# Transposing every second pair of attention rows in the scores' 64-row tiling, and scaling both layer-1 maxima with one product behind the reciprocal

## The reference

```python
sim = einsum('bihd,bjhd->bhij', q, k) * SCALE     # 112 x 375 per head
attn = softmax(sim, axis=-1)
out = einsum('bhij,bjhd->bihd', attn, v)
```

## Time and profile before

| | |
|---|---|
| median of 3 runs | 2443.48 us (2443.19 to 2444.84) |
| profiled execution | 2448.87 us, span 2447.0 us |
| busy share of the span | PE 97%, PEld 72%, DVE 68%, ACT 65%, POOL 67% |
| mean granted TensorE clock | 0.985 |
| attention pairs in all | 512 |

### The profile page before, as it was taken

The page is one execution under the profiler, slowest core; times in us unless marked ns, Lnnn a source line. Parts: engine busy times, 40 slices in busy tenths (PEclk is TensorE's granted clock), DMA queues, the critical chain, the costliest instruction groups (busy, mean ns, idle before and its releaser), DMA issues.

```text
span 2447.0 us, 58983 instructions
## 1 busy us (share of the span) xinstructions
PE 2369.9 (97%) x18734; PEld 1767.7 (72%) x18734; DVE 1658.4 (68%) x4412; ACT 1580.5 (65%) x4305; POOL 1648.5 (67%) x1894
## 2 busy tenths in 40 slices
PE   6999999999999999999999999999999999999578
PEld 5777777777777777777777777777777777777336
DVE  6666666776666667666666766666677666667775
ACT  4666666766666676666666766666676666666346
POOL 2666776666677766666776666677666666876507
PEclk9999999999999999999999999999999999999689
DMA  4100000000000000000000000000000000000202
GB/s 151 35 11 10 10 8 10 2 10 10 10 10 8 10 2 10 10 10 10 10 8 4 8 10 10 10 10 8 10 2 10 10 10 10 8 4 1 54 10 61
DMA packets 31196, 37.02 MB, mean 15 GB/s; under 512 B 3284, under 2 KB 29636, under 8 KB 31172
## 3 DMA queue, kind: packets, MB, share of 16 engines
q1 hardware_dynamic: 31172, 36.71, 5.1%
HBM read 29.36 MB, written 7.34 MB: 15 GB/s over the span
## 4 chain that ended last, share of the span: by engine, by line
PE 86%; ACT 5%; DVE 4%; issue 3%; POOL 1%; DMA 0%; ACTq 0%; POOLq 0%; DVEq 0%; SPq 0%
PE ps L334 24%; PE ps L395 15%; PE pt L405 14%; PE pa L417 5%; PE ps L378 5%; PE pa L452 5%; PE pa L432 4%; ACT prob L765 3%; PE pt L334 2%; PE pa L334 2%; PE pa L586 1%; PE pa L544 1%; DVE nmx L995 1%; PE pt L569 1%; PE ps L445 1%
## 5 line engine op out<-in xcount | busy, mean ns | idle before, releaser
L995 DVE TENSOR_REDUCE nmx<-ps 112x2 f32<-112x750 f32 x512 | 476.6, 936 | 204.1 <-PE ps L395 204.1
L1432 POOL TENSOR_TENSOR prob<-prob,rinv 112x375 f32<-112x375 f32 x512 | 404.2, 811 | 273.9 <-DVE rinv L1011 267.7
L1432 POOL TENSOR_TENSOR f1w_room<-f1w_room,rinv 112x375 f32<-112x375 f32 x512 | 404.8, 814 | 30.4 <-DVE rinv L1011 24.0
L727 ACT ACTIVATE room<-ps 128x375 f32<-128x375 f32 (+2 forms) x480 | 228.3, 489 | 272.2 <-PE ps L334 272.2
L986 DVE COPY probT<-pt 125x336 f32<-125x336 f32 x512 | 253.5, 495 | 100.0 <-PE pt L405 99.7
L727 ACT ACTIVATE probT<-pt 125x336 f32<-125x336 f32 x512 | 234.0, 457 | 109.0 <-PE pt L405 106.3
L405 PEld LDWEIGHTS pt<-ident,prob 112*125 112x125 f32 x1536 | 192.0, 189 | 130.3 <-issue 92.8
L405 PEld LDWEIGHTS pt<-ident,f1w_room 112*125 112x125 f32 x1536 | 197.9, 188 | 115.7 <-POOL f1w_room L1432 53.2
L1457 POOL TENSOR_TENSOR krs<-krs,nhalf 125x48 f32<-125x48 f32 x32 | 257.0, 8031 | 0.0
L405 PE MATMUL pt<-ident,prob 112*125 112x112 f32 x1536 | 239.6, 291 | 0.0
L405 PE MATMUL pt<-ident,f1w_room 112*125 112x112 f32 x1536 | 235.7, 287 | 1.6 <-DVE probT L986 0.9
(11 more groups left out here) (260 smaller groups left out, 5128.6 us busy)
## 6 DMA issues: line engine op xcount, KB each, us to landing
craw<-in_ctx SPq DMA_DIRECT2D x32, 375.0 KB, 3.1
xin<-in_x SPq DMA_DIRECT2D x32, 112.0 KB, 2.0
x_rows<-x SPq DMA_DIRECT2D x32, 112.0 KB, 1.9
out<-probT SPq DMA_DIRECT2D x16, 224.0 KB, 2.3
room<-x_rows SPq DMA_DIRECT2D x1, 2576.0 KB, 13.4
stage<-in_f1w SPq DMA_DIRECT2D x2, 1024.0 KB, 5.1
stage<-in_wk SPq DMA_DIRECT2D x1, 1024.0 KB, 7.8
stage<-in_wv SPq DMA_DIRECT2D x1, 1024.0 KB, 10.3
```

The source lines that it names most:

```text
L727: return act.activation(dst, src, ACT.Copy)
L995: top = dve.tensor_reduce(nmx[:, g:g + 2], ps[0:T, 2 * (i % 2):2 * (i % 2) + 2, 0:S], AX_X, ALU.max, negate=True)
L1432: pool.tensor_tensor(prob(i, n), prob(i, n), rinv[:, g:g + 1].to_broadcast([T, S]), ALU.mult).then_inc(s["normed"], 1)
```

## The change

Pairs with odd i and i+3 below the count (pairs 1, 3, 5, 7, 9, 11 of MIDDLE; 1 and 3 of OPENING and of CLOSING) are transposed by rows: each 112x125 piece becomes a transpose of its rows 0 to 63 into bank 0 and one of its rows 64 to 111 into bank 1, twelve transposes in place of six, behind a small bf16 product of one column. All waits stand ahead of that product: both copies of the pair before, and both heads' `normed`. ACT and DVE copy out one bank each as before, ACT 2x3x64 columns and DVE 2x3x48, both once all twelve are done. The other pairs stay as they are.

In layer 1 the two scalings become one 112x2 product (`max_scale`), which stands behind the reciprocal of the pair before in DVE's order and counts `maxed`; the maximum itself counts a new semaphore `top1`.

```diff
+        ROWS = ((0, 64), (64, T))
+        def by_rows(i, part):
+            return i % 2 == 1 and i + 1 + AHEAD < (G if part == MIDDLE else PAIRS)
...
             def turn(i, part, b):
+                if by_rows(i, part):
+                    pe.wait_ge(s["pT_even"], at(i, part, b))
+                    pe.wait_ge(s["pT_odd"], at(i, part, b))
+                    pe.wait_ge(s["normed"], 2 * at(i, part, b) + 2)
+                    pe.matmul(pt[:, 0, 511:512], identb[0:64, :], identb[0:64, 0:1], start=True, stop=True)
+                    for n in range(2):
+                        for t in range(KT):
+                            for bank, (r, e) in enumerate(ROWS):
+                                col = (n * KT + t) * (e - r)
+                                last = pe.transpose(pt[0:SK, bank, col:col + e - r],
+                                                    prob(i, n)[r:e, t * SK:(t + 1) * SK], ident[r:e, r:e])
+                                if n == 1 and t == KT - 1:
+                                    last.then_inc(s["pT"], 1)
+                    return
...
             def turned(i, part, b):
+                if by_rows(i, part):
+                    act.wait_ge(s["pT"], 2 * at(i, part, b) + 2)
+                    copy(probT[:, 2 * (i % 4):2 * (i % 4) + 2, :, 0:64],
+                         pt[0:SK, 0, 0:2 * KT * 64].rearrange("p (n k t) -> p n k t", n=2, k=KT))\
+                        .then_inc(s["pT_even"], 1)
...
-                if layer == 1:
-                    link(top)
-                    if p % 2 == 0:
-                        dve.wait_ge(s["q1_rstd"], b * 4 + (p // 2 + 1))
-                    for n in range(2):
-                        h = HEADS1[2 * p + n]
-                        top = dve.tensor_scalar(nmx[:, g + n:g + n + 1], nmx[:, g + n:g + n + 1], qrs[:, 2, h:h + 1],
-                                                None, ALU.mult)
-                top.then_inc(s["maxed"], 1)
+                top.then_inc(s["top1" if layer else "maxed"], 1)
+
+            def max_scale(i, part, b):
+                layer, p = pair_of(i, part)
+                if layer == 1:
+                    g, h = H + 2 * p, HEADS1[2 * p]
+                    assert HEADS1[2 * p + 1] == h + 4
+                    dve.wait_ge(s["top1"], b * PAIRS + (p + 1))
+                    if p % 2 == 0:
+                        dve.wait_ge(s["q1_rstd"], b * 4 + (p // 2 + 1))
+                    dve.tensor_tensor(nmx[:, g:g + 2], nmx[:, g:g + 2], qrs[:, 2, h:h + 5:4], ALU.mult)\
+                        .then_inc(s["maxed"], 1)
...
                     if i + 1 < count:
                         row_sum(i + 1, part, b)
+                    if i + AHEAD < count:
+                        max_scale(i + AHEAD, part, b)
```

More of the change, by code:

```diff
@@ L22 @@
 U8_EPS = 1e-8
-DVE_STEPS = 29
+DVE_STEPS = 21
 POOL_STEPS = 7
@@ L212, in xattn_ffn_kernel @@
             "x_in ctx_in cT_hi cT_lo k0_ready k0_sb v0_ready v0_sb var0 rstd0 xn0_ready xT0_ready xT0_sb "
-            "q0_ready q0_sb xbo_ready scores maxed exped recip normed pT pT_even pT_odd pv o_sb wo_ready x1_ready "
+            "q0_ready q0_sb xbo_ready scores top1 maxed exped recip normed pT pT_even pT_odd pv o_sb wo_ready x1_ready "
             "var1 rstd1 xq_ready diag_ready xqT_ready rb_ready xqT_sb rb_sb kv1_ready kv1_sb h_ready h_sb conv0 "
@@ L748, in turned @@
             def turned(i, part, b):
-                act.wait_ge(s["pT"], 2 * at(i, part, b) + 1)
-                copy(probT[:, 2 * (i % 4), :, :], pt[0:SK, 0, 0:KT * T].rearrange("p (k t) -> p k t", k=KT))\
-                    .then_inc(s["pT_even"], 1)
+                if by_rows(i, part):
[3 more added lines that the diff above has]
+                        .then_inc(s["pT_even"], 1)
+                else:
+                    act.wait_ge(s["pT"], 2 * at(i, part, b) + 1)
+                    copy(probT[:, 2 * (i % 4), :, :], pt[0:SK, 0, 0:KT * T].rearrange("p (k t) -> p k t", k=KT))\
+                        .then_inc(s["pT_even"], 1)
             def exps(i, part, b):
@@ L985, in turned @@
                 dve.wait_ge(s["pT"], 2 * at(i, part, b) + 2)
-                dve.tensor_copy(probT[:, 2 * (i % 4) + 1, :, :],
-                                pt[0:SK, 1, 0:KT * T].rearrange("p (k t) -> p k t", k=KT))\
-                    .then_inc(s["pT_odd"], 1)
+                if by_rows(i, part):
+                    dve.tensor_copy(probT[:, 2 * (i % 4):2 * (i % 4) + 2, :, 64:T],
+                                    pt[0:SK, 1, 0:2 * KT * (T - 64)].rearrange("p (n k t) -> p n k t", n=2, k=KT))\
+                        .then_inc(s["pT_odd"], 1)
+                else:
+                    dve.tensor_copy(probT[:, 2 * (i % 4) + 1, :, :],
+                                    pt[0:SK, 1, 0:KT * T].rearrange("p (k t) -> p k t", k=KT))\
+                        .then_inc(s["pT_odd"], 1)
             def row_max(i, part, b):
@@ L1217, in rest @@
                         row_max(i, CLOSING, b)
+                        max_scale(i, CLOSING, b)
                     row_sum(0, CLOSING, b)
```

## The result

The changed kernel takes 2436.71 us (median of 11, 2433.74 to 2441.89) against 2443.75 us (11 runs): ratio 0.9979, 95% interval 0.9971 to 0.9988. That is 7.0 us less where 21.2 were forecast: the right direction, inside the range, a third of the size.

A forecast was written before the change was run, and what follows sets the result against it. PE's own sequence was taken to bound the kernel. 0.65 us a pass over 31 passes gives 20.2 us, plus 1.0 for OPENING and CLOSING: 21.2 us less, median 2422.3 us, range 2411 to 2444.

The forecast's parts named there:

- Bound and block: PE's own sequence bounds; a by-rows block takes 1.37 us scores to scores instead of 1.65, saving 0.28.
- loads in series: Rival at L414: loads of the two halves go one after the other, or the tiling empties between; 2501 us, chance 0.13.
- The bare load behind the scores: Ahead of the by-rows transposes: first loads can't pass the small product, lie bare 0.10 us, first step at 0.82.
- the price of the scaling's product: Layer 1's 112x2 product on DVE, in no profile row: assumed 0.18 us, bounds 0.15 and 0.33.
- the forecast's sum: Whole kernel: 0.65 us a pass, 31 passes 20.2 us, OPENING and CLOSING 1.0; 21.2 us less, median 2422.3.
- GpSimd's chain swallows pairs 1 and 3: POOL's gapless chain over pairs 1 to 6 doesn't move, so anything won before is lost: gain 0 at scores 8.
- The walk from pair 8 on: Later MIDDLE pairs: gains 0.25 at scores 9, 0.31 at 10, 0.46 at 13; PE waits 0.4 before scores 11.
- The rival of a slow scaling behind the reciprocal: Layer 1: reciprocal's wait and ACT's later copies swallow most gain; 0.2 to 0.4 us a pass, 2431 to 2438, chance 0.23.
- Late copies at 0.05: Copies begin behind all twelve transposes and ACT copies more columns: costs 0.05 us where nothing else waits.

The follow-up runs named there:

- short roots: Against the changed kernel with layer 1's maxima in PSUM: GpSimd's four query roots a pass replaced by a subtraction; 2411.19 us, ratio to before 0.9863.
- maxima in PSUM: Against the changed kernel: layer 1's maxima written to spare PSUM columns, product still behind the reciprocal with one operand from PSUM; 2418.63 us, ratio to before 0.9900.
- two scalings behind: Against the changed kernel: the product replaced by two one-input scalings in the same place, behind the reciprocal; 2433.01 us, ratio to before 0.9957.

## Why the prediction was wrong

- **Bound and block: right; no loads in series.** 1.37 was forecast for scores to scores (1.65 before). Where nothing else is late, at pair 11, it is 1.32. At pair 5 it is 1.71, since the small product starts 0.88 after the scores and the exponentials of pair 7 end 0.05 before the next; without the standstill it is 1.39 there. At pair 7 the 1.41 ends with a wait for exponentials and is near the forecast partly by luck.
- **The bare load behind the scores: wrong, and to the good.** The small product did not hold the transposes' loads back: its load starts at 1175.01 and theirs at 1175.02, 0.58 after the scores' load and under the scores' stream, and the first transpose runs at 0.73 after the scores in place of 0.82. The twelve do go side by side in steps of 0.11, and half the rows save nothing in a load, as the prediction had it: 0.186 us at the median, against 0.188 with 112 rows before.

Weight loads of the changed kernel around that block:

```profile
1175.01 0.09 PEld L409 LDWEIGHTS pt<-identb 64*128 64x128 bf16 x1 [0.29 <-issue]
1175.02 0.88 PEld L414 LDWEIGHTS pt<-ident,f1w_room 48*125 48x125 f32 x12
1175.84 0.17 PEld L400 LDWEIGHTS ps<-kT,q 64*112 64x112 f32 x2
```

- **The failed step: the price of the scaling's product.** "bounds are the 0.15 of the 112x2 reciprocal and 0.33, that of the two scalings it replaces; I take 0.18". It took 0.14 to 0.16 for half of layer 1's pairs in a pass and 0.68 to 0.83 for pairs 4 to 7. The nearest rows by size were both one-input operations; what decides is that both operands lie in SBUF and that GpSimd is at work, which the earlier trace rows showed to be without a gap just there. Its upper bound had to be the rest of a GpSimd instruction, about 0.8 us. No rival had it. With the standstill removed and all else kept, the forecast's sum holds: 0.65 us a pass against 0.79 measured, 2422.3 against 2418.63 us, though not term by term, as the walk below shows.
- **GpSimd's chain swallows pairs 1 and 3: right for pair 3.** Scores 8 start at 17.25 to 17.27 in all kernels without a standstill that turn at most every second pair by rows, except with the short roots. Pair 1 had nothing to swallow: its block takes 1.66 in every kernel, since its small product starts 0.24 behind DVE's copy of pair 0, 0.96 after the scores.
- **The walk from pair 8 on**, held against the maxima in PSUM: scores 10 won 0.23 (0.31 forecast), scores 12 0.46 (0.26), scores 14 0.56. The distance of the exponentials of 8 and 9 was 1.69, not 1.88; the reciprocal and the product add less than their lengths, since each starts before the one ahead has ended. That PE would wait for the exponentials of 9 ahead of scores 11 came true: these start 0.05 behind their end.
- **The rival of a slow scaling behind the reciprocal** (0.33: 6 to 13 us won) describes the run with two scalings behind, 10.4 us, and its mechanism as well: the exponentials of 8 and 9 lie 1.87 apart there (2.03 by its own sum), and scores 11 and 13 wait for the exponentials of 9 and 11.
- **Late copies at 0.05**: nothing alone. Not in the walk was the hand-over from DVE's copy to the small product, 0.24 us. It decides the start of the block at pairs 1, 3, 5 and 9 of the changed kernel.

## What to carry over

Before swapping VectorE instructions, count their SBUF operands and look at what GpSimd does at that moment: an instruction ten times shorter than GpSimd's can last as long as GpSimd's does. Look at the least, median and most of an operation's length, not at its mean or its shape, and bound an unseen operation by what can block it. Keeping neighbouring products in one tiling saved up to 0.33 us a time here (1.65 to 1.32), as long as the copies of the block before are out when the next one begins and the exponentials are ready when it ends.

The best kernel of this study writes the maxima to spare PSUM columns: 2418.63 us behind the reciprocal and 2418.12 us ahead of it, 1.0% under the kernel before.

## What the hardware showed unexpectedly

A 112x2 product of two SBUF operands lasted 0.68 to 0.83 us beside a GpSimd multiplication and 0.14 to 0.16 us in its gaps, and 0.16 us beside it with one operand in PSUM. Weight loads of the next transposes started 0.01 us after that of the small product ahead of them, under the scores' stream, where before they had started bare at 0.82; what part the small product has in this was not tried. Twelve transposes of half the rows ran side by side in steps of 0.11 us, as long as six whole ones. An idle entry's releaser can be wrong where several waits stand together: the row named GpSimd 1.6 us after it was done.
